# The gated recurrence of block two takes decay and value from the layer-norm rows by a combined matrix, instead of from the projected input

## The chip, the cores and the metric

One core of a Trainium2 chip runs the whole program. The metric is device microseconds of one launch. Three runs of the kernel before took 937.53, 940.71 and 940.95 us; the median is 940.71 us.

## What is computed

Two pre-norm decoder blocks on x (16 sequences x 128 tokens x 128 features), each with a recurrence, a cross-attention and a feed-forward part. The change sits in the recurrence of block two and borrows time in the feed-forward part of block one (eight experts and a shared one). Cut to what matters, the recurrence is:

```python
def _L1_attn_ref(x, omega, Win, Wl, bl, Wv, bv, Wout):      # x is the layer norm of the residual
    xz = jnp.einsum('btd,ed->bte', x, Win)
    xi, z = jnp.split(xz, 2, axis=-1)                       # 256 features each
    log_lam = -C * softplus(omega) * sigmoid(jnp.einsum('bti,ji->btj', xi, Wl) + bl)
    lam = jnp.exp(log_lam)
    v = jnp.einsum('bti,ji->btj', xi, Wv) + bv
    h0 = xi[:, 0]
    def step(h_prev, inp):
        x_t, v_t, lam_t = inp
        vh = jnp.sum(v_t * h_prev, axis=-1, keepdims=True)
        vv = jnp.sum(v_t * v_t, axis=-1, keepdims=True)
        Qh = h_prev - 2.0 * v_t * (vh / vv)
        h = lam_t * Qh + (1.0 - lam_t) * x_t
        return (h, h)
    ...
    return jnp.einsum('bti,di->btd', silu(z) * h, Wout)
```

## The kernel before, in words

Everything lies in SBUF with features on the 128 partitions. The 2048 token rows form four groups g of 512. The five engines each run one hand-written order of instructions and meet by counting semaphores.

**Rounded products.** Where single precision is wanted at the fast rate, a matrix is kept in two parts of type fp32r, an upper part (a rounded copy) and a lower part (the rest). A product is then three fast ones (PARTS: upper x upper, upper x lower, lower x upper) accumulated in PSUM. `up` (L1751) does this with the parts of the layer-norm rows in `xhl` and of the weights in `whl`. Plain fp32 products of 128x512 show as two records each.

**The expert loop of block one** (TensorE, ScalarE and VectorE each loop over i = 0 to 35: nine feed-forward networks times four groups). A step is four times `up` (12 fast products), Silu on ScalarE (`silu_up`, L821), the gate product on VectorE (`hidden`, L1300), upper and lower part of the hidden rows (`hidden_upper` L828, `hidden_lower` L1308), and the down product of the step before (`down_T`, L1925, 6 fast products; L1744 in steps 4 to 7 and 32 to 35). VectorE also adds the weighted outputs (L1317, L1322). TensorE waits in step i for the Silu and gate product of step i - 1, bank by bank. PSUM banks 0 to 5 are used; 6 and 7 serve the router and the last transposes.

**The stage before the recurrence** (this is what the change reorders). The last layer norm of the block runs group by group: `normalize(3, g)` (L664) on ScalarE and L1056 on VectorE, `transpose_xn(3, g)` on TensorE into bank g, `copy_xnT(3, g)` (L673, upper part) on ScalarE and `ln_lower` (L1064, lower part) on VectorE. Then:

- `xz(g)`: 12 fast products into banks 4 to 7, one bank per 128 features (the first half is xi, the second z). `xz_copy(g)` (L860) on ScalarE copies each to SBUF.
- `lam_or_v` (L1999): from xi in SBUF, full fp32, two products of contraction 128 for each 128 output features; v goes to banks 0 and 1, lambda to 2 and 0. It waits for the first two `xz_copy` of its group.
- ScalarE: v with its bias (L875), its square (L880), tanh (L883) and exp (L887) for lambda. Tanh is in the table that Silu left; exp isn't, so a table load stands before the first exp.
- `v_dot_v(g)` (L2011) sums the squares into bank 3; VectorE takes the reciprocal (L1415); `spread_reciprocal(g)` (L2017) brings it to all partitions, again in bank 3.
- VectorE, for each group: nb = (lambda - 1) * xi (L1418), w = -2 v / vv (L1421), w * lambda (L1424), then `chain_products(g)` (L1378 to L1385): products of lambda, v and w over the positions 1 to 3 of chunks of four tokens. For g = 1 it writes into R[2], which lies on rows of `xhl`, and so waits until all 16 products of xz are done.
- GpSimd, for each group: local sums gl, their products with v (L552 to L566). For g = 1 it waits for all 16 `xz_copy`.
- `chunk_dots(g)` (L2035, L2039): sums of the chain products over features into banks 4 to 7 (0 to 3 for g = 3). The first waits for all 16 `xz_copy`. ScalarE copies a part (`e_copy`, L868); VectorE's `solve(g)` (L1401 to L1409) follows, one group behind its chain products.

TensorE's order today is xz(0), then for g = 0 to 3: v and lambda of g, v_dot_v(g), spread_reciprocal(g); behind g = 0 come xz(1) and xz(2), behind g = 1 xz(3) and the dots of group 0, and so on. The recurrence itself (32 chunks, L1470 to L1486 with L2078) follows.

## Time and profile before

| | |
|---|---|
| median of three runs | 940.71 us (937.53 to 940.95) |
| the profiled execution, its span | 947.1 us, 6.4 us above that median; the page gives nothing around the span |
| busy, of the span | TensorE 812.7 us (86%), weight loads 583.1 (62%), VectorE 768.9 (81%), ScalarE 524.0 (55%), GpSimd 492.0 (52%) |
| expert loop of block one | about 300 to 466 us |
| stage before the recurrence | 471.7 us to about 556 us |
| recurrence of block two | about 556 to 626 us |
| costliest group | L1751, 576 fast products, 145.3 us busy |
| L1308, lower part of the hidden rows | 56 instructions, 806 ns mean |

How to read it: a share of busy time is an average over stages with different limits, so the chain that ended last (which piece of work released the next) is read together with the timelines of the engines in the two stretches. TensorE's records overlap, so the time from one start to the next says more than the length of one. The granted clock is a share of TensorE's full speed.

### The profile page before, as it was taken

How to read it: one execution, taken by the hardware profiler on the slowest of the kernel's cores; microseconds unless marked ns; L12 is line 12 of the kernel's file. 1: busy time of each engine (PE TensorE's matmuls, PEld its weight loads, DVE VectorE, ACT ScalarE, POOL GpSimd, SP SyncE). 2: the span in 40 equal slices, each digit the busy share in tenths (PEclk: the TensorE clock that was granted, in tenths of full speed). 3: DMA queues.
4: the chain of work that ended last, by engine and by line, in shares of the span. 5: the costliest groups of instructions: out<-in, count | busy, mean ns of one | idle time of the engine just before them, and what ended most of it. 6: DMA issues, size and time to landing. Idle time of an engine off the chain costs nothing.

```text
span 947.1 us, 14667 instructions
## 1 busy us (share of the span) xinstructions
PE 812.7 (86%) x5061; PEld 583.1 (62%) x5061; DVE 768.9 (81%) x1419; ACT 524.0 (55%) x960; POOL 492.0 (52%) x490
## 2 busy tenths in 40 slices
PE   7958777777798999999999867799999899899891
PEld 6433232322266888887866555577766678789781
DVE  5588999999987489999848988886799978857663
ACT  5966666666637635554364232226565684078771
POOL 6358999999962021222248833456344310077773
PEclk9968999999998899999999999999799999999996
DMA  7000000000000031323000000000000031096554
GB/s 205 1 0 1 0 1 1 0 1 0 0 1 1 12 114 62 106 79 106 0 2 1 1 0 1 1 1 1 1 2 25 24 89 47 14 163 173 152 128 158
DMA packets 36739, 39.67 MB, mean 42 GB/s; under 512 B 5131, under 2 KB 28697, under 8 KB 35898
## 3 DMA queue, kind: packets, MB, share of 16 engines
q1 hardware_dynamic: 34170, 33.62, 11.8%
q0 software_dynamic: 2496, 5.12, 3.3%
q8 instruction: 40, 0.66, 0.3%
q14 instruction: 33, 0.27, 0.1%
HBM read 30.86 MB, written 7.86 MB: 41 GB/s over the span
## 4 chain that ended last, share of the span: by engine, by line
PE 39%; DVE 19%; ACT 5%; issue 5%; POOL 4%; DMA 3%; POOLq 0%; ACTq 0%; SPq 0%; DVEq 0%
PE ps L1751 10%; PE ps L1925 3%; PE ps L1744 3%; PE ps L2132 2%; DMA G<-xn_rows,token 2%; PE ps L1999 2%; PE ps L2267 2%; POOL y_rows L640 2%; DVE small L1520 2%; PE ps L2122 1%; PE ps L2276 1%; PE ps L2078 1%; DVE R L1481 1%; PE ps L1799 1%; DVE G L1523 1%
## 5 line engine op out<-in xcount | busy, mean ns | idle before, releaser
L1751 PE MATMUL ps<-xhl,whl 128*128 128x512 f32 x576 | 145.3, 402 | 5.3 <-ACT G L701 2.6
L1751 PEld LDWEIGHTS ps<-xhl,whl 128*128 128x128 f32 x576 | 109.0, 193 | 30.1 <-issue 5.7
L476 POOL TENSOR_TENSOR R<-G,R 128x1024 f32<-128x1024 f32 x43 | 100.8, 2360 | 28.9 <-ACT R L707 22.5
L1189 DVE TENSOR_TENSOR_SCAN R<-ps,R 128x1024 f32<-128x1024 f32 x43 | 97.5, 2278 | 5.5 <-POOL R L485 5.5
L749 ACT ACTIVATE ps<-G,negAb,negA 128x508 f32<-128x508 f32 x128 | 95.0, 779 | 2.6 <-DVE R L1189 2.6
L1778 PE MATMUL ps<-bc,sel 96*128 96x512 bf16 x128 | 47.1, 396 | 51.5 <-ACT LN L714 22.1
L1799 PE MATMUL ps<-R,ident 128*128 128x512 f32 x172 | 83.1, 605 | 0.0
L1778 PEld LDWEIGHTS ps<-bc,sel 96*128 96x128 bf16 x128 | 12.5, 99 | 104.7 <-ACT LN L714 35.8
L707 ACT COPY R<-ps 128x512 f32<-128x512 f32 x64 | 37.5, 585 | 71.1 <-PE ps L1778 71.1
L821 ACT ACTIVATE G<-ps 128x512 f32<-128x512 f32 x72 | 42.8, 599 | 56.7 <-PE ps L1751 56.6
L440 POOL TENSOR_TENSOR rstd<-small,mhalf 128x4 f32<-128x4 f32 x24 | 25.7, 1069 | 86.4 <-DVE small L1050 86.4
L635 POOL DMA_INDIRECT G<-xn_rows,token x39 | 39.4, 1010 | 58.9 <-DVE per_tile L1683 45.4
L1300 DVE TENSOR_TENSOR G<-G,ps 128x512 f32<-128x512 f32 x72 | 48.6, 681 | 17.1 <-ACT G L821 16.2
L445 POOL CAST whl<-ew 128x512 fp32r<-128x512 f32 x9 | 5.8, 646 | 106.5 <-DMA ew<-in_w_dram 106.4
L965 ACT COPY G<-ps 120x512 f32<-120x512 f32 x64 | 34.9, 589 | 42.0 <-PE ps L2132 42.0
L1693 DVE TENSOR_TENSOR G<-ps,biasT 128x512 f32<-128x512 f32 x39 | 26.9, 690 | 34.8 <-PE ps L2267 34.7
L1799 PEld LDWEIGHTS ps<-R,ident 128*128 128x128 f32 x172 | 32.5, 194 | 29.1 <-issue 24.0
L1189 DVE TENSOR_TENSOR_SCAN LN<-ps,LN 128x1024 f32<-128x1024 f32 x21 | 47.9, 2280 | 2.7 <-POOL LN L485 2.1
L476 POOL TENSOR_TENSOR LN<-G,R 128x1024 f32<-128x1024 f32 x21 | 49.8, 2373 | 0.1
L1729 PE MATMUL ps<-ident 128*128 128x128 f32 x326 | 42.8, 291 | 5.8 <-DVE G L1407 3.3
L1308 DVE TENSOR_TENSOR hl<-G,hl 128x512 fp32r<-128x512 f32 x56 | 44.6, 806 | 1.9
L1729 PEld LDWEIGHTS ps<-ident 128*128 128x128 f32 x326 | 40.9, 206 | 7.2 <-DVE G L1407 3.9
(376 smaller groups left out, 2162.8 us busy)
## 6 DMA issues: line engine op xcount, KB each, us to landing
R<-in_exp_wi_dram SPq DMA_DIRECT2D x39, 256.0 KB, 3.5
G<-cw_by_expert SPq DMA_DIRECT2D x6, 1024.0 KB, 4.6
ew<-in_w_dram SPq DMA_DIRECT2D x24, 128.0 KB, 2.2
y_rows<-zeros SPq DMA_DIRECT2D x1, 2048.0 KB, 9.3
xn_rows<-LN SPq DMA_DIRECT2D x8, 256.0 KB
G<-in_exp_wo_dram SPq DMA_DIRECT2D x8, 256.0 KB, 4.7
G<-y_rows SPq DMA_DIRECT2D x4, 512.0 KB, 5.5
X<-in_x_dram SPq DMA_DIRECT2D x4, 256.0 KB, 4.6
```

Of the source, the lines that this page charges most:

```text
L476: gp.tensor_tensor(halves(dBu[i % 3]), duT[:, :, gcols(i // NS)], Bsb[:, i % 4:i % 4 + 1, :].broadcast_to([P, HI, GT]), ALU.mult).then_inc ...
L635: gp.indirect_dma_start(x_at(i), None, xn_dram[:, :], bass.IndirectOffsetOnAxis(ap=token[:, i:i + 1], axis=0))\
L707: sc.copy(Bsb[:, i % 4, :], bank(4)[:, 0, :]).then_inc(S["b_copied"], 1)
L749: sc.activation(bank(2 * j + m)[:, 0, :].rearrange("p (b t) -> p b t", b=GB)[:, :, 1:T], dT[:, m, gcols(g)].rearrange("p (b t) -> p b t", ...
L821: sc.activation(sh[:, i % 2, m * GT:(m + 1) * GT], bank(m)[:, 0, :], ACT.Silu).then_inc(S["silu0"], 1)
L1189: v.tensor_tensor_scan(hst[i % 3], bank(2 * j, 2).rearrange("p h n -> p (h n)"), dBu[i % 3], 0.0, ALU.mult, ALU.add).then_inc(S["scanned"], 1)
L1300: v.tensor_tensor(hidr[:, i % 2, m * GT:(m + 1) * GT], sh[:, i % 2, m * GT:(m + 1) * GT], bank(2 + m)[:, 0, :], ALU.mult).then_inc(S["hid0 ...
L1308: v.tensor_tensor(hl[:, i % 2, 1, m * GT:(m + 1) * GT], hidr[:, i % 2, m * GT:(m + 1) * GT], hl[:, i % 2, 0, m * GT:(m + 1) * GT].bitcast( ...
L1729: mm(bank(o)[:, 0, 0:P], ident[:], ident[:], start=True, stop=True)
L1751: ins = mm(mix(out) if n == N_WIN1 else out, whl[:, wslot(n), i, m * P:(m + 1) * P], rhs, start=k == 0, stop=k == 2)
L1778: mm(bank(bank_i)[:, 0, :], sel[:, r, :], bc3[:, gcols(g)], start=True, stop=True).then_inc(S[s], 1)
L1799: ins = mm(bank(6 + m)[:, 0, :], ident[:], hC[i % 3][:, m * GT:(m + 1) * GT], start=False, stop=i % NS == NS - 1, skip_group_check=True)
```

## The change

- Before the loop's end, a combined matrix is made: the first half of the input projection (Win's xi rows) is transposed on TensorE at step 11 into bank 7, ScalarE copies it (step 12), TensorE multiplies it with Wv and Wl at step 13 in full fp32 (four products of 128x256) into bank 6, ScalarE writes the upper part (step 14) and VectorE the lower (step 15). The result `lvhl` (128 x 2 parts x 512) takes the place of weights of block one that are no longer needed.
- v and lambda are three fast products of `lvhl` with `xhl` for each 128 features, and no longer wait for xz or its copies; they wait for the group's layer-norm parts and their banks.
- The order of TensorE and ScalarE in the stage is new. VectorE's nb now waits for the group's xi copies. The table with exp and tanh is loaded ahead of the last normalizations.

```diff
...
 DRIVE = 4
 NDRIVE = NC // DRIVE
 FIRST_ROUND = (10, 18, 26)
+LV_AT = 11
 POOL_HC = (1, 4, 7, 10, 13)
 EB = 4
 NT = 2 * N // P + E - 1
...
         nones, nselu = diagD[:, 0, :], diagD[:, 1, :]
         rvv = sb("rvv", [P, NG, C4])
 
+        with nc.sbuf_tensor("lvhl", [P, 2, 2 * DI], F32R) as lvhl:
+            pass
+
         w = {}
         for name, shape in (
             ("W_in", [P, 4, P]), ("W_delta", [P, HI, DI]), ("b_delta", [P, HI]), ("W_BC", [P, HI, 2 * NS]),
...
         wo_now = R[:, 3, :, :].rearrange("p s (w n) -> p (s w) n", w=2)
 
 
+        Win1T = LN[:, 1, 0:HI * P].rearrange("p (k n) -> p k n", k=HI)
+
         S = {}
         for name in (
             "x_in0", "x_in1", "x_in2", "x_in3", "w_win", "w_mamba", "w_ctx", "w_lru", "w_att", "w_gate", "w_e0a", "w_e0b",
...
 
         FIRST = {}
         for name, shared, count in (
+            ("wt1_mm", "cwt_mm", 1), ("wt1_ev", "rt_exp", 1), ("lv_mm", "rt_mm", 1), ("lv_hi", "rt_cw", 1), ("lv_lo", "rt_sub", 1),
             ("bc_up", "w_upper", 1), ("bc_rem", "diag_ready", HI), ("sp_log", "omega_sp", 1),
             ("t_mm", "l_mm", HI * NG), ("cnt_mm", "vt_mm", NG), ("lst_mm", "vv_mm", NG), ("bt_mm", "dots_mm", 2 * NG), ("wo_cp", "z_silu", 2 * HI), ("ebo_mm", "hk_mm", NG),
             ("xt_ev", "l_ev", HI * NG), ("bt_ev", "lam_done", HI * NG), ("ebo_ev", "v2_ev", HI * NG),
...
                 if i == 2 * NG - 1:
                     act.wait_ge(S["cwt_mm"], 1)
                     sc.copy(cw_rows, bank(6)[:, 0, 0:T]).then_inc(S["cw_rows"], 1)
+                if i == LV_AT + 1:
+                    wait(act, "wt1_mm", 1)
+                    sc.copy(Win1T, bank(7)[:, 0, 0:HI * P].rearrange("p (k n) -> p k n", k=HI)).then_inc(S["wt1_ev"], 1)
+                if i == LV_AT + 3:
+                    wait(act, "lv_mm", 1)
+                    sc.copy(lvhl[:, 0], bank(6)[:, 0, :]).then_inc(S["lv_hi"], 1)
                 if i == 3:
                     act.wait_ge(S["rt_sub"], 1)
                     sc.activation(router[:, 1, :, :], router[:, 0, :, :], ACT.Exp).then_inc(S["rt_exp"], 1)
 
+            sc.preload_act_table_set("exp_and_others")
             for g in range(NG):
                 normalize(3, g)
                 if g == NG - 2:
...
                 act.wait_ge(S["dots_mm"], 2 * g + 2)
                 sc.copy(row(cp, g)[:, 1:C4], e_psum(g).rearrange("p (i k) -> p i k", k=KG)).then_inc(S["e_ev"], 1)
 
-            xz_copy(0)
             copy_xnT(3, NG - 1)
-            for g in range(NG):
+
+            def v_copy(g):
                 for m in range(HI):
                     act.wait_ge(S["v2_mm"], HI * g + m + 1)
                     sc.activation(row(vv[:, m], g), mix(bank(m)[:, 0, :]), ACT.Identity, bias=w["bv"][:, m:m + 1])\
                         .then_inc(S["v2_ev"], 1)
+
+            def v_square(g):
                 act.wait_ge(S["v2_ev"], HI * (g + 1))
                 if g >= 2:
                     act.wait_ge(S["vt_mm"], g - 1)
                 sc.activation(sq[:, g % 2], pos(vv, g), ACT.Square).then_inc(S["sq_done"], 1)
+
+            def decays(g):
                 for m in range(HI):
                     act.wait_ge(S["l_mm"], HI * g + m + 1)
                     sc.activation(row(lam[:, m], g), mix(bank(2 - 2 * m)[:, 0, :]), ACT.Tanh, bias=coef[:, 0, m:m + 1], scale=0.5)\
...
                     act.wait_ge(S["l_ev"], HI * g + m + 1)
                     sc.activation(row(lam[:, m], g), row(lam[:, m], g), ACT.Exp, bias=coef[:, 2, m:m + 1], scale=coef[:, 2, m:m + 1])\
                         .then_inc(S["lam_done"], 1)
-                if g == 0:
-                    xz_copy(1)
-                    xz_copy(2)
-                if g == 1:
-                    xz_copy(3)
-                if g >= 1:
-                    carry_last(g - 1)
-                    e_copy(g - 1)
+
+            for g in range(NG):
+                v_copy(g)
+                if g < NG - 1:
+                    v_square(g)
+                decays(g)
+                xz_copy(g)
+            carry_last(0)
+            e_copy(0)
+            v_square(NG - 1)
+            for g in range(1, NG - 1):
+                carry_last(g)
+                e_copy(g)
             carry_last(NG - 1)
             e_copy(NG - 1)
             for m in range(HI):
...
                 elif i == NG + 1:
                     compare(probs, range(E // 2, E))
                     step(v.tensor_reduce(router[:, 2], pair[:, 0], AX.X, ALU.add))
+                if i == LV_AT + 4:
+                    wait(dve, "lv_hi", 1)
+                    v.tensor_tensor(lvhl[:, 1], bank(6)[:, 0, :], lvhl[:, 0].bitcast(F32), ALU.subtract).then_inc(S["lv_lo"], 1)
                 if 0 <= i - E * NG + 1 < NG:
                     add_YT(i - E * NG + 1)
                 if i > E * NG:
...
                 v.reciprocal(rvv[:, g, :], bank(3)[:, 0, 0:C4 * VW:VW]).then_inc(S["rvv_done"], 1)
                 dve.wait_ge(S["lam_done"], HI * (g + 1))
                 step(v.memset(lam_g[:, :, 0, 0:GB], 0.0))
+                dve.wait_ge(S["xz_ev"], 4 * g + HI)
                 v.scalar_tensor_tensor(pos(nb, g), lam_g, 1.0, pos(xi, g), ALU.subtract, ALU.mult).then_inc(S["nb_done"], 1)
                 dve.wait_ge(S["nb_done"], g + 1)
                 dve.wait_ge(S["vv_mm"], g + 1)
...
                 if i == 2 * NG - 1:
                     pe.wait_ge(S["rt_cw"], 1)
                     nc.tensor.transpose(bank(6)[:, 0, 0:T], router[:, 5].rearrange("p b e -> p (b e)"), ident[:]).then_inc(S["cwt_mm"], 1)
+                if i == LV_AT:
+                    pe.wait_ge(S["w_lru"], 16 * 6)
+                    for k in range(HI):
+                        ins = nc.tensor.transpose(bank(7)[:, 0, k * P:(k + 1) * P], w["Win1"][:, k, :], ident[:])
+                    ins.then_inc(S["wt1_mm"], 1)
+                if i == LV_AT + 2:
+                    wait(pe, "wt1_ev", 1)
+                    for j, name in enumerate(("Wv", "Wl")):
+                        for k in range(HI):
+                            ins = mm(bank(6)[:, 0, j * DI:(j + 1) * DI], Win1T[:, k, :], w[name][:, k, :], start=k == 0, stop=k == HI - 1)
+                    ins.then_inc(S["lv_mm"], 1)
                 if i - 1 in by_feature:
                     down_T(i - 1)
                 elif i >= 1:
...
             pe.wait_ge(S["w_split"], N_WIN1 + 1)
 
             def xz(g):
-                pe.wait_ge(S["ln_lo"], 2 * NG + g + 1)
-                if g == 0:
-                    pe.wait_ge(S["res0"], (E + 1) * NG)
                 for m in range(4):
                     if g:
                         pe.wait_ge(S["xz_ev"], 4 * g - 3 + m)
                     up(bank(4 + m)[:, 0, :], N_WIN1, m, g).then_inc(S["xz_mm"], 1)
 
-            def lam_or_v(g, wt, banks, done, freed):
+            def lam_or_v(g, first, banks, done, freed):
 
                 for m in range(HI):
                     if freed[m][1] > 0:
                         pe.wait_ge(S[freed[m][0]], freed[m][1])
-                    for k in range(HI):
-                        ins = mm(mix(bank(banks[m])[:, 0, :]), wt[:, k, m * P:(m + 1) * P], row(xi[:, k], g),
-                                 start=k == 0, stop=k == HI - 1)
+                    elif banks[m]:
+                        pe.wait_ge(S["ln_lo"], 2 * NG + banks[m] + 1)
+                    cols = slice((first + m) * P, (first + m + 1) * P)
+                    for k, (i, j) in enumerate(PARTS):
+                        ins = mm(mix(bank(banks[m])[:, 0, :]), lvhl[:, i, cols], row(xhl[:, j], g), start=k == 0, stop=k == 2)
                     ins.then_inc(S[done], 1)
+
+            def lam_and_v(g):
+                pe.wait_ge(S["ln_lo"], 2 * NG + g + 1)
+                lam_or_v(g, 0, (0, 1), "v2_mm", (("l_ev", HI * g), ("v2_ev", HI * g)))
+                lam_or_v(g, HI, (2, 0), "l_mm", (("l_ev", HI * g - 1), ("v2_ev", HI * g + 1)))
 
             def v_dot_v(g):
                 pe.wait_ge(S["sq_done"], g + 1)
...
                     ins = mm(e_psum(g), ones[:], ep[g % 2][:, k], start=k == 0, stop=k == HI - 1)
                 ins.then_inc(S["dots_mm"], 1)
 
+            wait(pe, "lv_lo", 1)
+            pe.wait_ge(S["res0"], (E + 1) * NG)
+            transpose_xn(3, NG - 1)
+            lam_and_v(0)
             xz(0)
-            transpose_xn(3, NG - 1)
-            for g in range(NG):
-                pe.wait_ge(S["xz_ev"], 4 * g + HI)
-                if g == 0:
-                    pe.wait_ge(S["ln_lo"], 2 * NG + 3)
-                lam_or_v(g, w["Wv"], (0, 1), "v2_mm", (("l_ev", HI * g), ("v2_ev", HI * g)))
-                lam_or_v(g, w["Wl"], (2, 0), "l_mm", (("l_ev", HI * g - 1), ("v2_ev", HI * g + 1)))
+            v_dot_v(0)
+            spread_reciprocal(0)
+            lam_and_v(1)
+            xz(1)
+            v_dot_v(1)
+            lam_and_v(2)
+            xz(2)
+            lam_and_v(3)
+            xz(3)
+            spread_reciprocal(1)
+            chunk_dots(0)
+            for g in range(2, NG):
                 v_dot_v(g)
                 spread_reciprocal(g)
-                if g == 0:
-                    xz(1)
-                    xz(2)
-                if g == 1:
-                    xz(3)
-                if g:
-                    chunk_dots(g - 1)
+                chunk_dots(g - 1)
             chunk_dots(NG - 1)
 
             def s_known(c):
```

## Rows read from the trace of the kernel before

**Rows 1.** The chain that ended last, pieces in order: start us, us, what
```profile
413.88 2.72 PE ps L1751 x12
416.60 1.36 PE ps L1925 x6
...
471.72 3.01 PE ps L1751 x12
...
475.17 6.87 PE ps L1999 x16
482.04 1.75 PE ps L2011 x16
...
484.04 1.16 PE ps L2017 x8
485.20 5.46 PE ps L1751 x24
...
504.13 2.87 PE ps L2035 x12
```

**Rows 2.** Busy time by stretch, core 0: us, each engine's busy us, granted clock, DMA
```profile
376.00:399.00 23.00, 23.00 (x104) 19.02 (x103) 22.45 (x35) 13.39 (x24) 3.84 (x4) 1.00 0.21 67
534.00:535.00 1.00, 1.00 (x8) 1.00 (x9) 1.00 (x1) 0.00 (x0) 0.00 (x0) 0.70 0.00 0
535.00:536.00 1.00, 1.00 (x4) 0.70 (x4) 0.55 (x2) 0.00 (x0) 0.73 (x1) 0.50 0.00 0
538.00:540.00 2.00, 2.00 (x11) 1.59 (x10) 1.97 (x2) 0.00 (x0) 1.90 (x2) 1.00 0.00 0
```

**Rows 3.** Timeline of VectorE: start us, us, line, operation, [idle before, releaser]
```profile
385.23 2.59 DVE L1308 TENSOR_TENSOR hl<-G,hl 128x512 fp32r<-128x512 f32 x2
...
485.76 1.23 DVE L1418 SCALAR_TENSOR_TENSOR G<-G 128x1024 f32<-128x1024 f32 x1
...
499.29 0.18 DVE L1415 RECIPROCAL rvv<-ps 128x4 f32<-128x4 f32 x1 [2.69 <-PE ps L2011]
...
501.27 1.22 DVE L1421 SCALAR_TENSOR_TENSOR G<-G,ps 128x1024 f32<-128x1024 f32 x1
...
503.86 0.96 DVE L1378 TENSOR_TENSOR R<-G 128x768 f32<-128x768 f32 x1
...
516.92 0.18 DVE L1415 RECIPROCAL rvv<-ps 128x4 f32<-128x4 f32 x1 [1.26 <-PE ps L2011]
...
518.71 1.22 DVE L1421 SCALAR_TENSOR_TENSOR G<-G,ps 128x1024 f32<-128x1024 f32 x1
...
521.47 1.36 DVE L1378 TENSOR_TENSOR ew<-G 128x768 f32<-128x768 f32 x1
...
535.51 1.22 DVE L1421 SCALAR_TENSOR_TENSOR G<-G,ps 128x1024 f32<-128x1024 f32 x1 [0.45 <-PE ps L2017]
```

**Rows 4.** Timeline of ScalarE in the second block
```profile
461.34 0.87 ACT L664 ACTIVATE LN<-X,stats,rstd 128x128 f32<-128x128 f32 x2
...
467.91 1.05 ACT L673 CAST xhl<-ps 128x512 fp32r<-128x512 f32 x2
...
472.75 2.60 ACT L860 COPY G<-ps 128x512 f32<-128x512 f32 x4 [1.52 <-PE ps L1751]
...
482.78 1.28 ACT L887 ACT_TABLE_LOAD   x1
...
512.48 1.06 ACT L880 ACTIVATE LN<-G 128x1024 f32<-128x1024 f32 x1
...
515.19 0.69 ACT L883 ACTIVATE G<-ps,coef 128x512 f32<-128x512 f32 x1 [1.03 <-PE ps L1999]
515.78 1.50 ACT L887 ACTIVATE G<-G,coef 128x512 f32<-128x512 f32 x2
```

**Rows 5.** Timeline of TensorE in the second block
```profile
465.01 0.82 PE L1737 MATMUL ps<-ident,LN 128*128 128x128 f32 x6
...
533.83 1.57 PE L2017 MATMUL ps<-ident,rvv 128*128 128x128 f32 x8 [3.02 <-DVE rvv L1415]
```

## The prediction, made before the changed kernel was run

> **What bounds the kernel now.** I read the chain that ended last first, then the busy time by stretch, then the timelines of TensorE, ScalarE, VectorE and GpSimd between 456 and 556 us. Two places matter, because the change adds work in one and reorders the other.
>
> The first is the expert loop of block one (steps i = 0 to 35). From i = 9 on, the chain is TensorE alone: 12 products of L1751 in 2.72 us, then 6 of L1925 in 1.36 us, so a step every 4.08 us [rows 1]. TensorE is busy 23.00 of 23.00 us there, VectorE 22.45, ScalarE 13.39 [rows 2]. Work put on TensorE here moves the end by its own length.
>
> The second is the stage before the recurrence of block two, from 471.72 [rows 1] to about 556 us. For each of four groups TensorE makes xz (12 rounded products, 2.73 us, half of the 5.46 us for two groups), then v and lambda (L1999, 16 records, 6.87 us), the sums of squares (L2011, 1.75 us) and the spread reciprocal (L2017, 1.16 us) [rows 1]. Until 515 us the chain lies almost wholly on TensorE, after that on VectorE. Once fed, VectorE stops only briefly: 1.26 us before the reciprocal of group 2 and 0.45 us before w of group 3 [rows 3].
>
> **The change, part by part.**
>
> (a) Expert loop, TensorE. Four transposes took 0.44 us (475.17 less 471.72 + 3.01 [rows 1]), so the two at i = 11 cost 0.22. At i = 13, four full-precision products 128 columns by 256 are 8 records. A 512-column record of L1999 takes 6.87/16 = 0.43 us, so a 256-column one takes 0.215 us, and eight take 1.72 us [rows 1]. Sum 1.94 us, all on the path. Bounds: 0 if TensorE had slack (the stretch shows none), 2.6 if the switches between forms cost 0.1 us each. I take 1.95.
>
> (b) Expert loop, other engines. ScalarE gets two copies of about 0.6 us; it is idle 9.6 us in 23 [rows 2], and the copies stand behind its last work of a step, so nothing. VectorE gets one subtraction of about 0.7 us. It is nearly full [rows 2], but when GpSimd stretched two of its ops to 2.59 us [rows 3], 1 us over their mean on the page, TensorE kept its step; and TensorE has just stood 1.94 us longer, which VectorE gains as slack. I take 0; if that cover were gone, 0.7.
>
> (c) The table load. Today it stands between tanh and exp of group 0, 1.28 us [rows 4]. It moves ahead of the first normalization, which starts at 461.34 us and takes 0.87 [rows 4]. That one then ends near 463.6 instead of 462.2 us; its transposes start at 465.01 us behind other products [rows 5]. Cost 0.
>
> (d) The order of the stage. v and lambda become 3 rounded products for each 128 rows, as in xz: 2.73 us a group in place of 6.87, so 4 x 4.14 = 16.6 us leave TensorE. Were TensorE the only limit, that would be the gain. It isn't: three waits stand in the new code. The spread reciprocal of group 1 is issued after xz of group 3. VectorE's chain products of group 1 wait for all 16 xz products, since they write where the rows xhl lie. The first dots wait for all 16 copies of xz, since they use the same banks. So I lay out the new times on the old clock.
>
> TensorE is free at 471.4. Transposes of group 3 take 0.44 us, so lambda and v of group 0 run 471.85 to 474.6, xz to 477.35, squares and the wait for VectorE's reciprocal take 2.0 us (482.04 to 484.04), the spread 1.16 [rows 1]: 480.5. The first v of group 1 is in ScalarE's hands at 481.3.
>
> ScalarE then sets the pace. One group is two v activations (0.6 and 0.7, as tanh), the square (1.06), two tanh (0.69, but 0.59 from one start to the next, 515.19 to 515.78), two exp (1.50) [rows 4], and four copies of xz. The four took 2.60 us where TensorE delivered one each 0.68 us; two copies that lay ready took 1.05 us together, so four ready ones take 2.1 [rows 4]. A group is 7.0 us (7.5 with the slow copies). Two groups on from 481.3, with a small wait on TensorE at group 2: 495.65. Its first v activation of group 3 ends at 496.3 and frees bank 0; then TensorE makes the last lambda product (0.68), xz of group 3 (2.73, ends 499.75) and the spread (1.16). VectorE can start w of group 1 at **501.0**. It starts at 501.27 today [rows 3]. With 7.5 us a group it would be 502.0.
>
> So VectorE, which begins group 0 near 479.6 instead of 485.76 (it needs the reciprocal at 479.4 and xi), has finished that group at 490.4 and nb of group 1 at 492, and stands idle for 9 us. The 16.6 us saved on TensorE are mostly a wait.
>
> From w of group 1 on VectorE is again the bound. Today 501.27 to 515.66 us (516.92 less its wait of 1.26), 14.4 us [rows 3]. Its ops that ran while GpSimd was idle will now run beside it, for GpSimd starts group 1 once all xz copies are out, as the first dots do: near 502 us, and not at 504.1 [rows 1]. The first chain product took 0.96 us there against 1.36 us beside GpSimd in group 2 [rows 3], and the product before it can lose some 0.3 (estimate from that pair). So 14.4 + 0.7 = 15.1, and group 2's reciprocal comes at 516.1 against 516.92.  Now something new is late: TensorE has had nothing since about 508 us, 8 us of idleness.
>
> (e) The clock. Today group 3's spread follows 3.02 us of idleness and takes 1.57 us for 1.16 [rows 5]; the granted clock is 0.70 in its last part, then 0.50 [rows 2]: the 1.2 GHz level. VectorE waits 0.45 us for that spread [rows 3]. In the new order group 2's spread comes after 8 us of idleness. At full clock w of group 2 starts near 517.4, with a spread twice as slow (2.3 us) at 518.6; today 518.71 [rows 3]. Group 3 can lose another 0.5 us in the same way. The whole stage changes by -1.3 to +1.0 us; I take **-0.4**, between the two, as only the last part of today's spread ran slow. The Trainium skill (TensorE: Matmul & The Clock Gate, Part 1) has the engine at 1.2 GHz by default and released by activity; by it both spreads run at half clock from the start, and the stage comes out at +0.5. Trace and page differ on the first part of that spread only.
>
> The dots of groups 1 to 3 (2.87 us for 12 records [rows 1], about 4 for all 16) run beside VectorE's chain products and have some 4 us of room before its solve, so they cost nothing unless the clock stays low. The recurrence behind the stage is untouched: TensorE is warmed for it by the same products.
>
> Sum: +1.95 - 0.4 = **+1.6 us** on this execution, whose span of 947.1 us lies 6.4 us above the median of the three runs (940.71); nothing beside the span is shown for it, so I carry the difference over: 942.3.
>
> **Rivals.**
>
> R1, VectorE stays fed. If, against my reading, VectorE could run group 1 straight behind group 0, the stage would end earlier by its 6.15 us head start and by its later stalls (2.69 + 1.26 + 0.45 = 4.4 [rows 3]): -10.6 + 1.95 = -8.6, 932.1. For it: that is what shorter products would do, and v and lambda stand on today's chain with 6.87 us a group. Against it: both waits of (d) are in the code, and even a stage bound by TensorE alone (eight times 2.73, two rounds of squares, one spread, the transposes) ends xz of group 3 at 498.4, so w of group 1 not before 499.6. Chance 0.09.
>
> R2, slower: the low clock lasts. It decides if TensorE stays at 1.2 GHz through the dots of groups 1 and 2 and not for about 3 us as today. Then dots take 8 us instead of 4 and use up their room. Two spreads cost 1.2 us more each, two dots up to 0.5 each, and VectorE's subtraction of (b) 0.7, against 1.0 us saved ahead of them: 1.95 + 2.4 + 1.0 + 0.7 - 1.0 = +5, 945.8. For it: TensorE's busy share falls from near full to half in the stage. Against it: from 538 us on the clock is back at 1.00 today [rows 2]. Chance 0.12.
>
> R3, the added products are hidden, or take no time, in the expert loop: -0.4, 940.3. Against it, a chain that is all TensorE. Chance 0.07.
>
> Forecast as above: 0.72.
>
> **How the numbers follow.** About 0.5% (4.7 us) is what a measurement of this kernel can tell from no change. My own case spans -1.3 + 1.9 = +0.6 to 1.0 + 2.7 = +3.7 us; a start of w 1 us later takes it to +4.7, and the runs before lie 3.4 us apart, so its upper end is 945.5. The 8 in 10 range reaches down through R3 to 938.8 and up to 946.0, into R2. Faster: R1, 0.09. Slower: R2, 0.12. Within: 0.79.
>
> **What would show it.** In the profile after: 8 records of about 0.215 us between two steps of the loop, and the loop 1.95 us longer (wrong if the steps absorb them); no table load between tanh and exp; VectorE's first op of group 0 some 6 us earlier on the stage's clock, and a gap of 8 to 10 us ahead of w of group 1, released by the spread reciprocal; the first dots within 2 us of today's place; granted clock 0.5 somewhere in the spreads of groups 2 and 3. The prediction is wrong if that gap is under 4 us, or if ScalarE isn't dense from 481 to 499 us.

## The result, and the profile after

The changed kernel took 947.24 us (median of four executions, 946.35 to 948.34), the kernel before 939.38 us beside it (937.53 to 940.95). The ratio is 1.0085, with an interval of 1.0064 to 1.0105: 7.9 us slower. I had forecast 942.3 us, and a range that ends at 946.0. The profiled execution has a span of 944.9 us (946.65 us with what lies around it), shorter than the 947.1 us of the trace I had read of the kernel before. That is the first thing to explain, and it is taken up behind the table below.

What I had laid out by hand is in the trace nearly as written. First the added work in the expert loop, in the timeline of TensorE (start us, us, line, operation):

```profile
351.98 2.89 PE L1778 MATMUL ps<-xhl,whl 128*128 128x512 f32 x12
354.70 0.38 PE L1992 MATMUL ps<-ident,w_Win 128*128 128x128 f32 x2
354.84 1.64 PE L1952 MATMUL ps<-hl,w2hl 128*128 128x512 f32 x6
...
363.12 1.02 PE L1998 MATMUL ps<-w_Wv,LN 128*128 128x256 f32 x4
363.98 1.03 PE L1998 MATMUL ps<-w_Wl,LN 128*128 128x256 f32 x4
364.66 1.74 PE L1952 MATMUL ps<-hl,w2hl 128*128 128x512 f32 x6
```

The first set of four records takes 0.86 us from its start to the start of the next (363.12 to 363.98). A record is 0.215 us, as worked out, and TensorE never stops around them.

Then the stage, as TensorE saw it (the same view, 468 to 533 us):

```profile
468.88 0.63 PE L1764 MATMUL ps<-ident,LN 128*128 128x128 f32 x4
469.26 3.02 PE L2037 MATMUL ps<-xhl,lvhl 128*128 128x512 f32 x12
472.13 2.89 PE L1778 MATMUL ps<-xhl,whl 128*128 128x512 f32 x12
...
490.92 2.26 PE L2037 MATMUL ps<-xhl,lvhl 128*128 128x512 f32 x9
493.87 0.96 PE L2037 MATMUL ps<-xhl,lvhl 128*128 128x512 f32 x3 [0.69 <-ACT G L889]
494.67 2.89 PE L1778 MATMUL ps<-xhl,whl 128*128 128x512 f32 x12
497.39 1.05 PE L2059 MATMUL ps<-ident,rvv 128*128 128x128 f32 x8
498.94 2.87 PE L2077 MATMUL ps<-ew,ones 128*128 128x384 f32 x12 [0.50 <-ACT G L874]
...
513.62 2.07 PE L2059 MATMUL ps<-ident,rvv 128*128 128x128 f32 x8 [8.78 <-DVE rvv L1441]
...
530.79 2.08 PE L2059 MATMUL ps<-ident,rvv 128*128 128x128 f32 x8 [8.15 <-DVE rvv L1441]
```

v and lambda of a group now take 2.87 us from start to start, for 6.87 before [rows 1]. The last lambda product waits for ScalarE, as reckoned. And TensorE stands idle for 8.78 and 8.15 us ahead of the last two spread reciprocals, which take 2.07 and 2.08 us; in the kernel before the last one took 1.57 [rows 5]. VectorE (its timeline, same columns) shows what that does:

```profile
477.03 1.23 DVE L1445 SCALAR_TENSOR_TENSOR G<-G 128x1024 f32<-128x1024 f32 x1
...
498.55 1.22 DVE L1448 SCALAR_TENSOR_TENSOR G<-G,ps 128x1024 f32<-128x1024 f32 x1 [8.97 <-PE ps L2059]
...
501.34 1.30 DVE L1404 TENSOR_TENSOR R<-G 128x768 f32<-128x768 f32 x1
...
513.39 0.17 DVE L1441 RECIPROCAL rvv<-ps 128x4 f32<-128x4 f32 x1
...
515.80 1.22 DVE L1448 SCALAR_TENSOR_TENSOR G<-G,ps 128x1024 f32<-128x1024 f32 x1 [0.95 <-PE ps L2059]
```

It waits 8.97 us in front of w of group 1; I had said 9. From the transposes of group 3 to that w are 29.7 us; I had said 501.0 less 471.4 = 29.6. The granted clock is still 1.00 when TensorE falls idle, goes to 0.50 within each idle stretch and stays there through the spread:

```profile
503.00:508.00 5.00, 1.83 (x17) 1.69 (x15) 4.86 (x6) 1.73 (x3) 4.69 (x6) 1.00 0.00 0
508.00:518.00 10.00, 4.38 (x12) 3.22 (x13) 8.76 (x16) 0.00 (x0) 8.24 (x12) 0.50 0.00 1
518.00:525.00 7.00, 4.64 (x29) 3.82 (x27) 6.83 (x7) 0.78 (x2) 6.76 (x7) 0.98 0.00 0
525.00:535.00 10.00, 4.21 (x12) 3.22 (x13) 8.76 (x16) 0.00 (x0) 6.88 (x10) 0.50 0.00 0
```

(Busy time by stretch of the changed kernel, columns as in rows 2.) So nothing in the stage accounts for 7.9 us. Cut into parts, by the starts of the same products in each trace, the two executions compare so:

| trace | expert loop, from the down product of step 8 to the last one | from there to the last layer norm's transposes | stage, to the first recurrence product | recurrence | attention heads of block two, first to last score product |
|---|---|---|---|---|---|
| before, the trace read for the prediction | 95.30 | 18.56 | 91.70 | 62.47 | 106.49 |
| changed | 97.16 | 18.81 | 91.78 | 62.46 | 106.45 |

The change costs 1.86 + 0.25 + 0.08 = 2.2 us. In these two traces the heads are alike. What I did not know is that 106.5 us is not what they take at their best. The trace of before already showed the clock low in them (busy time by stretch, columns as in rows 2; its first score product starts at 653.50 us):

```profile
653.50:660.50 7.00, 5.01 (x43) 3.71 (x42) 6.82 (x9) 3.46 (x5) 7.00 (x11) 1.00 0.00 1
660.50:667.50 7.00, 6.91 (x53) 4.70 (x54) 6.35 (x6) 3.57 (x6) 2.33 (x6) 0.51 0.01 2
667.50:674.50 7.00, 7.00 (x56) 5.19 (x55) 2.17 (x4) 2.66 (x4) 2.56 (x6) 0.51 0.00 0
```

Why is the changed execution the shorter one all the same? Its down product of step 8 starts at 346.54 us, that of before at 351.15, and up to there the two kernels do the same. From the down product of step 1 to that of step 8 the changed kernel's trace takes 39.30 us and that of before 42.49. In the latter the clock was at 0.50 from 316 to 322 us. The router's products and the down product behind them show it, in TensorE's timeline of before:

```profile
312.86 4.01 PE L1914 MATMUL ps<-w_router,LN 128*128 128x8 f32 x32
316.73 2.91 PE L1925 MATMUL ps<-hl,w2hl 128*128 128x512 f32 x6
```

and in that of the changed kernel:

```profile
311.45 3.63 PE L1941 MATMUL ps<-w_router,LN 128*128 128x8 f32 x32
314.94 1.63 PE L1952 MATMUL ps<-hl,w2hl 128*128 128x512 f32 x6
```

In the 20 traces of this case this piece has one of three lengths, whatever the kernel: 39.3 to 39.4 us in seven, 40.9 to 41.0 in six, 42.5 to 42.6 in seven. So executions of one program reach the later stages up to 3.2 us apart by this alone.

In four of the five later sets of runs the routed experts at the end, in which TensorE waits for token rows brought by DMA (8.1 us in all in h2's trace), took 118 to 130 us from their first product on TensorE to their last, instead of 95 to 97, and scattered, so the times there are near 967 us and are only compared with the kernel before beside them.

### The profile page after: what moved, and what is told of

Read it like the earlier page. It is cut to its first block, busy times and chain, and to the rows that moved or that the text cites. A ratio compares the mean times of both kernels' runs of the same rounds, so it can differ in the third digit from the quotient of the medians.

```text
span 944.9 us, 14658 instructions
## 1 busy us (share of the span) xinstructions
PE 792.9 (84%) x5055; PEld 577.0 (61%) x5055; DVE 771.4 (82%) x1420; ACT 521.3 (55%) x962; POOL 493.4 (52%) x490
## 4 chain that ended last, share of the span: by engine, by line
PE 32%; DVE 24%; issue 6%; ACT 5%; POOL 5%; DMA 2%; POOLq 0%; DVEq 0%; ACTq 0%
PE ps L1778 7%; PE ps L1771 3%; POOL y_rows L647 2%; PE ps L2177 2%; DVE G L1323 2%; PE ps L2167 2%; DVE small L1547 2%; POOL G L642 2%; PE ps L1952 2%; PE ps L2312 2%; DVE G L1550 1%; PE ps L2123 1%; DVE R L1508 1%; DMA G<-xn_rows,token 1%; PE ps L1826 1%
## 5 line engine op out<-in xcount | busy, mean ns | idle before, releaser
L1778 PE MATMUL ps<-xhl,whl 128*128 128x512 f32 x576 | 143.0, 397 | 6.0 <-ACT G L708 2.6
L483 POOL TENSOR_TENSOR R<-G,R 128x1024 f32<-128x1024 f32 x43 | 100.8, 2359 | 26.7 <-ACT R L714 20.4
```

Source lines behind the costliest of these rows:

```text
L483: gp.tensor_tensor(halves(dBu[i % 3]), duT[:, :, gcols(i // NS)], Bsb[:, i % 4:i % 4 + 1, :].broadcast_to([P, HI, GT]), ALU.mult).then_inc ...
L1778: ins = mm(mix(out) if n == N_WIN1 else out, whl[:, wslot(n), i, m * P:(m + 1) * P], rhs, start=k == 0, stop=k == 2)
```

## The experiments

### First set: before again, the matrix alone, the spread earlier, the load where it was

**b1**, the kernel before, unchanged. 

> The kernel before, unchanged, profiled again. Theory S (the stage and the expert loop behave as the trace of before showed, but that one execution was itself slow somewhere outside them): the span comes out near 938 us, the stage from the last transposes to the first recurrence chunk takes the same 85 us as in the first trace of before, and the 8 to 10 us between the traces lie elsewhere. Rival T (the first trace was typical in its shape, and before's other executions are shorter in the stage): the stage itself is several us shorter than 85 us here.

Measured 967.37 us against 966.91 (1.0013, 0.998 to 1.0045). In its trace the loop takes 95.28 us, the stage 91.73, the heads 106.51. Theory S holds for the stage, and rival T falls (with before's order the stage takes 91.5 to 92.3 us in all five traces). But the heads are long again, so this trace doesn't yet show where before's usual executions are shorter.

**e1**, the kernel before with the combined matrix made and not used. Cut to the two places on TensorE:

```diff
+                if i == LV_AT:
+                    ...
+                if i == LV_AT + 2:
+                    ...
```

> The combined matrix is made in the expert loop as in the changed kernel, but not used; the stage is that of before. Theory A (TensorE is the chain in the loop, the work is on it): 1.95 us over before, within 1.5 to 2.7. Rival L (the added work sets TensorE's clock or the engines' phase off and costs several times its length somewhere later): 5 us or more over before, with a lower mean clock.

Measured 1.0027 (0.9991 to 1.0064), or 2.6 us with 3.5 either way. The trace is sharper: the loop takes 97.14 us, 1.86 more than b1. The stage takes 92.31 us, 0.6 more than in b1, though its code is that of before. And the heads take 98.41 us, 8.1 less, in code that nothing touched.

**e2**, the changed kernel with one line moved.

```diff
             xz(2)
+            spread_reciprocal(1)
             lam_and_v(3)
             xz(3)
-            spread_reciprocal(1)
```

> The changed kernel, with the spread reciprocal of group 1 issued ahead of lambda and v of group 3 and not behind xz of group 3. By the trace of the changed kernel VectorE waits about 8 us for it, and its chain products of group 1 wait for xz of group 3 alone. Theory A: w of group 1 and its product with lambda leave the path, the stage ends 3 to 4 us sooner than in the changed kernel: about 943.5 us. Rival: another wait (dots or solve of group 0) takes its place, and the gain is under 1 us.

Measured 0.9944 (0.991 to 0.9978) of before. The stage is 87.60 us, 4.2 under the changed kernel. VectorE's timeline (same columns):

```profile
492.30 1.22 DVE L1448 SCALAR_TENSOR_TENSOR G<-G,ps 128x1024 f32<-128x1024 f32 x1 [2.48 <-PE ps L2059]
...
497.81 0.96 DVE L1404 TENSOR_TENSOR R<-G 128x768 f32<-128x768 f32 x1 [2.59 <-PE ps L1778]
```

The wait of 8.97 us became two, of 2.48 us for the spread and of 2.59 us for xz of group 3. This was theory A.

**e3**, the changed kernel without the early table load.

```diff
-            sc.preload_act_table_set("exp_and_others")
```

> The changed kernel without the early load of the exp and tanh table, so that the load stands again between tanh and exp of group 0. Theory A: ScalarE is dense to xz of group 3, so the stage grows by at most 1.3 us over the changed kernel, unless its first wait of 0.7 us for group 1 absorbs part: 947.5 to 948.5 us. Rival L (what is lost lies in the loop's end, where the early load delays the layer norm): no change or a gain against the changed kernel.

The stage stays at 91.78 us. ScalarE waits 0.27 us for the first v of group 1 and not 1.70 us: that wait had room for the load, so the early load gains nothing and costs nothing. Yet the kernel measured 1.0073 of before (1.0033 to 1.0112), and eight of its ten executions had a mean granted clock of 0.940 to 0.945 (seven of these took 970 to 979 us), the other two 0.950 and 0.952 at 967 and 965 us. Its trace is one of the latter, with heads of 98.41 us. Executions like the seven are called the long kind below. That their heads took 106.5 us is a guess for all that have no trace.

### Second set: are the heads the place?

TensorE has two gaps at the start of the heads, while VectorE and ScalarE work on the first scores. The edit fills them; `unread(bank, n)` issues n full fp32 products of 128 x 128, whose results nobody reads:

```diff
             head_scores(0, 1)
+            unread(4, 3)
             pe.wait_ge(S["hq_lo"], NG)
-            unread(7, 8)
+            unread(7, 13)
```

**f1**, the changed kernel again. 

> The changed kernel, unchanged, against before on one chip, with a second profile. Theory C (the change itself costs about 0.9 us of schedule, and the rest of the 7.9 us was the attention heads of block two starting at the 1.2 GHz level, 106.5 against 98.4 us, which this kernel's executions meet more often than those of before): the ratio lies between 1.001 and 1.009, and its runs split by mean clock, about 0.01 apart. Rival R (the 7.9 us are in the change's own stage and the traces hide it): the ratio is 1.0085 again and the runs do not split.

1.0058 of before (1.0027 to 1.0089), median 972.0 us. The traced execution took 964.58 us with heads of 98.43 us at a mean clock of 0.950; the other eleven took 970 to 978 us, at clocks of 0.934 to 0.947.

**f2**, the changed kernel with the fill. 

> The changed kernel with eight more unread products on TensorE in the two gaps at the start of the attention heads (3 before the wait for the last query part, 13 in place of 8 behind it). Theory C: the heads take 98.4 to 99 us in the profile and the median falls by up to 8 us against the changed kernel. Rival: the clock falls all the same and the heads take 106 us or more.

0.9993 (0.9959 to 1.0028): 4.2 us under f1. In the trace the clock holds at the start of the heads and is at 0.50 later, from 725 to 730 us; they take 101.1 us.

**f3**, the kernel before with the fill. 

> The kernel before with the same eight more products. Theory C: its heads take 98.4 to 99 us; it gains at most as much as before's executions met the low clock there, and stands 0.9 us under the changed kernel with the same products (a ratio of the two of 1.001). Rival R: the changed kernel stays 5 us or more behind it.

0.9969 (0.9939 to 0.9999), heads 100.8 us. The two filled kernels stand 2.6 us apart, close to the 2.2 us of schedule, where the unfilled ones stood 5.7 apart. Rival R falls, and the stage of 91.8 us in every trace of the changed kernel says the same. The heads did not come down to the forecast 99 us in either: by the times the fill helps the changed kernel (f2 against f1), and it doesn't cure.

**f4**, fill and early spread. 

> Both: the early spread reciprocal of group 1 and the eight more products. Theory A with C: the stage 4.1 us shorter than in the changed kernel and the heads at 98.4 to 99 us; the fastest of all, 3 us or more under before with the same products.

0.9941 (0.991 to 0.9973), stage 87.62 us, heads 99.7 us. It is the fastest of the set, 2.5 us under f3, where 3 or more had been expected.

### Third set: is it the moment at which the heads come?

The edit is idle products on TensorE at step 15 of the expert loop, in front of everything in question: `unread(7, 4)`, `(7, 5)`, `(7, 9)`.

**g1**, the kernel before with 0.9 us more. 

> The kernel before with four unread products (8 records, 0.9 us) more on TensorE at step 15 of the expert loop: as much longer, up to the heads, as the changed kernel's trace is. Theory P (whether the attention heads start at the 1.2 GHz level hangs on the moment at which they come, and the change moved them by about 0.9 us): it is slow like the changed kernel, 4 us or more over before, with a mean clock about 0.005 lower. Rival Q (the slow heads come from what the changed order does in its stage, its idle TensorE and its low clock there): 0.9 us over before and no more.

0.9992 (0.9964 to 1.002): theory P missed, and so did the 0.9 us, which the scatter on this chip hides (the loop is 0.92 us longer in the trace, the heads 101.1 us).

**g2**, the changed kernel with 1.1 us more. 

> The changed kernel with five unread products (1.1 us) more at step 15. Theory P: most of its executions get past the low clock in the heads, so it is 3 to 7 us faster than the changed kernel beside it although it does 1.1 us more work. Rival Q: 1.1 us slower than the changed kernel.

0.9999 (0.9972 to 1.0025), 967.75 us, and no execution at a clock under 0.948. The changed kernel beside it (g4) stood at 975.7 us. With more work it was 8 us faster by the median (5.5 by the mean), and its trace has heads of 98.39 us; rival Q says slower by 1.1.

**g3**, with 2.05 us more. 

> The changed kernel with nine unread products (2.05 us) more at step 15. Theory P: as the one with five, or between it and the changed kernel. Rival Q: 2 us slower than the changed kernel.

1.0035 (1.0011 to 1.0059), clocks from 0.943 to 0.955: between g2 and g4. Its traced execution took 974.01 us at a clock of 0.943, which looks like the long kind, and yet its heads took 98.41 us. Its down product of step 8 started at 351.80 us, 3.3 us behind that of g2's trace. So in these scattered sets neither the time nor the mean clock of an execution tells what its heads did.

**g4**, the changed kernel. 

> The changed kernel unchanged, as the reference on this chip. Theories P and Q alike: 4 to 8 us over before; the loop's 97.1 us and the stage's 91.8 us in the profile as in the two traces before, and heads of either 98.4 or 106.5 us.

1.0054 (1.0014 to 1.0095). Five of eight executions took 975 to 979 us at clocks of 0.938 to 0.942, the other three 963 to 969 us at 0.950 to 0.953. The traced one is of these, with heads of 98.41 us.

### Fourth set: TensorE kept busy in the stage

**h1** and **h2**, two more traces of the changed kernel, in a set as quiet as the first measurement. 

> A further profile of the changed kernel. If it falls among the slow executions (mean clock about 0.942), theory C expects the loss in the attention heads (106.5 for 98.4 us) with loop 97.1 and stage 91.8 us as before; rival Q expects the stage or the recurrence to be longer than 91.8 and 62.5 us.

> As the one before it: theory C, any loss against 98.4 us is in the heads; rival Q, in the stage or the recurrence.

h1 took 942.72 us with heads of 100.94 us and a mean clock of 0.952; h2 took 940.77 us with 98.41 us and 0.961. Loop and stage are alike in both (97.1 and 91.8 us). The kernel before had 939.94 us beside them (17 executions, 937.65 to 941.20, clocks 0.962 to 0.967).

**h3**, the changed kernel with its two idle stretches filled.

```diff
             for g in range(2, NG):
                 v_dot_v(g)
+                unread(0, 34)
                 spread_reciprocal(g)
```

> The changed kernel with 34 unread products on TensorE in each of its two idle stretches of 8 us ahead of the spread reciprocals of groups 2 and 3. In the profile both spreads run at full clock and VectorE's waits of 0.95 us for them go: the stage is 1 to 2 us shorter (theories P and Q alike). Theory Q (idleness and low clock of the stage bring the slow executions on): the slow group vanishes, 5 us or more under the changed kernel, at or under before. Theory P (it is the moment at which the heads come that decides): the median moves by the 1 to 2 us and by whatever the shift does, in either direction.

939.10 us, 0.9993 of before (0.9983 to 1.0002), twelve executions between 937.75 and 940.92 us, clocks 0.962 to 0.969. TensorE's timeline:

```profile
509.24 7.81 PE L1756 MATMUL ps<-ident 128*128 128x128 f32 x68
518.21 1.16 PE L2059 MATMUL ps<-ident,rvv 128*128 128x128 f32 x8 [1.16 <-DVE rvv L1441]
...
534.60 1.16 PE L2059 MATMUL ps<-ident,rvv 128*128 128x128 f32 x8 [1.97 <-DVE rvv L1441]
```

Both spreads are back at 1.16 us, the stage is 90.25 us, 1.5 less, and no execution is of the long kind; its trace has heads of 98.41 us. But neither h1 nor h2, all there is of the changed kernel beside it, was of that kind. So the set shows the 1.5 us of the stage, and that before's time is reached; that h3 took the long kind away follows only against the first measurement.

**h4**, early spread, filled stage (19 products ahead of group 2's spread, 34 ahead of group 3's) and filled heads. 

> Early spread reciprocal of group 1, TensorE kept busy in the stage, and the eight more products at the heads. Theory A with C: stage 86 to 87 us, heads 98.4 to 100 us, no slow group, and 0.6 to 0.9% faster than before.

935.68 us, 0.9961 of before (0.9948 to 0.9974): 4.3 us under the kernel before, stage 86.84 us, heads 98.40 us. The forecast of 0.6 to 0.9% was too high.

### Last set: busy TensorE, same moment

**i1**, h3 with seven products (1.6 us) at step 15, so that the heads come when they do in the changed kernel. 

> The changed kernel with TensorE kept busy in the stage (34 unread products twice) and seven unread products (1.6 us) more at step 15 of the expert loop, so that the heads come at the moment at which they come in the changed kernel. Theory Q (idleness and low clock of the stage bring the slow heads on): still no slow group, 1.6 us over the version without the seven products. Theory P (the moment decides): the slow group is back, and the median is within 2 us of the changed kernel.

**i2**, the changed kernel beside it. 

> The changed kernel beside it. Both theories: 4 to 8 us over before, executions in two groups by clock.

i1 measured 965.76 us, 1.0035 of before (1.0004 to 1.0066), i2 970.27 us (1.0056, 1.0027 to 1.0085). i1 scatters again: six executions of 961 to 965 us, six of 966 to 972, with no gap between them; its trace has a stage of 90.23 us and heads of 100.90. That is not the even kernel that theory Q expects, and its median is 4.5 us under i2's, not within the 2 us of theory P. With ranges of 10.6 and 12.0 us in twelve executions each, this set does not decide between them.

i2's trace caught an execution with long heads in the changed kernel, beside one with short heads (h2). Its execution took 973.35 us at a mean clock of 0.940, one of the long kind, and its loop, stage and recurrence are 97.11, 91.79 and 62.46 us, as in all the others. The heads take 106.51 us. Busy time from their first product on, i2:

```profile
652.30:659.30 7.00, 5.00 (x43) 3.70 (x42) 6.82 (x9) 3.47 (x5) 7.00 (x11) 1.00 0.00 1
659.30:666.30 7.00, 6.91 (x53) 4.68 (x54) 6.35 (x6) 3.56 (x6) 2.33 (x6) 0.51 0.01 2
666.30:673.30 7.00, 7.00 (x56) 5.18 (x55) 2.18 (x4) 2.66 (x4) 2.54 (x6) 0.51 0.00 0
673.30:680.30 7.00, 7.00 (x108) 5.20 (x112) 5.47 (x8) 4.83 (x8) 2.59 (x6) 1.00 0.01 2
```

and the same 28 us of h2, the same program:

```profile
653.30:660.30 7.00, 5.03 (x43) 3.71 (x42) 6.82 (x9) 3.43 (x4) 7.00 (x11) 1.00 0.00 1
660.30:667.30 7.00, 6.33 (x90) 4.63 (x94) 6.69 (x7) 5.35 (x9) 3.49 (x10) 1.00 0.01 2
667.30:674.30 7.00, 7.00 (x116) 5.38 (x109) 5.86 (x7) 4.08 (x7) 3.59 (x8) 1.00 0.01 2
674.30:681.30 7.00, 6.90 (x102) 5.20 (x102) 6.88 (x9) 4.71 (x8) 3.00 (x7) 1.00 0.00 0
```

After the same seven microseconds with TensorE 5.0 us busy, one execution goes on at 1.00 and the other at 0.51, nearly all of it at the 1.2 GHz level, for the next 14 us. There TensorE is full and issues about half as many records, and VectorE, nearly full in h2, is left waiting: 2.2 us busy in the third stretch instead of 5.9. Single groups of products show it too. These are two lines of TensorE's timeline in the changed kernel's first trace; just before, the same kinds of products, as many of them, took 0.92 and 1.09 us:

```profile
658.11 1.54 PE L2167 MATMUL ps<-kz,qhl 32*128 32x480 f32 x6
659.61 1.96 PE L2177 MATMUL ps<-ident,G 128*120 128x128 f32 x8
```

## Why the prediction was wrong

**(a), the added products: right.** 1.86 us for 1.95, and no switch between forms cost anything that shows. **(b)**, the copies and the subtraction at nothing: right, the loop grew by TensorE's part alone. **(c)**, the table load: right that it costs nothing where it went, and it saved nothing where it left (e3), because ScalarE had a wait of 1.70 us to hide it in. The 0.25 us between loop and transposes come with the matrix (18.81 us in e1 too, 18.57 in b1); their cause was not looked for.

**(d), the order: right.** The start of w, the 8.97 us of idleness and ScalarE's pace were in the trace to 0.1 us, and e2 showed what the wait for the spread had cost: moved forward by one line it gave 4.2 of the 16.6 us by which TensorE's products had become shorter. (By the lengths as the prediction lists them, ScalarE's group adds up to 7.2 us and not 7.0; from start to start it took 7.1 on average.) R1 fell, as its waits are real: even in e2 VectorE waits 2.59 us for xz of group 3.

**(e), the clock in the stage: right in kind, a little small.** The spreads took 2.07 and 2.08 us, and VectorE waited 0.95 us for each (h3 brought both back to 1.16 us and took 1.5 us off the stage). The stage came out at +0.1 us, for my -0.4: w of group 2 came 0.4 us earlier than before, as seen from the start of the stage, and the longer wait for group 3's spread, 0.95 for 0.45 us, took that back. The upper bound of +1.0 us does not follow from its own terms, which give +0.4. The Trainium skill's rule (TensorE: Matmul & The Clock Gate, Part 1) was the better guide here: by it both spreads run at half clock from the start, and they did.

The sum of these is +2.2 us, for my +1.6. An execution of the changed kernel whose heads were not slowed took 940.77 us, and before took 939.94 us beside it.

**The step that failed is that all behind the stage was put at nothing, with "The recurrence behind the stage is untouched" as its only reason.** The recurrence is (62.46 for 62.47 us), but I ended the search there. The heads, 97 us behind the stage, took 98.4 us at their best and 106.5 us when the clock fell to its lower level at their start. In the two quiet sets (the first measurement and the fourth set) the times say that this is common in the changed kernel and rare in the one before: the former took 946.35 us or more in four of six executions, the latter 941.20 us or less in all 21, and only the execution traced for the prediction was longer. The traces by themselves don't: with the kernels unchanged, the heads were long in both traces of before and in two of six of the changed kernel (98.4 us in three, 100.9 in one). The rival R2 named the right cause, a low clock that lasts, at the wrong place: it priced it in the stage.

**A second step was weak: how the execution stands to the median.** I noted that the profiled span lay 6.4 us above the median of the runs, and wrote "I carry the difference over" without asking where it was. It was in the heads. That trace had 106.49 us in a kernel whose usual time has room for 98.4 only. Had I looked at the clock of the stretches behind the stage, the lower level at the start of the heads would have stood out, and its price could have been estimated. As it was, 942.3 us came near to the executions whose heads were not slowed so (940.77 and 942.72 us), which is what it had been worked out for.

Do the other executions of the first measurement fit? They have no traces. Their mean clocks, 0.951, 0.950 and 0.953, are like that of the trace with long heads (0.953), but h1 has 0.952 with heads of 100.94 us, so the clock doesn't decide it. Their times do better: 946.4 to 948.3 us, beside 946.65 for the trace, and 3.6 to 5.6 us above h1. With h2's 940.8 us and heads longer by 8.1 one gets 948.9 us, from which the pieces ahead of step 8 can take some 2 us, as in the trace. So all four probably had the loss; this is argued and not shown.

**What stays open** is why the change would make this fall of the clock common. Two things seem to move it. With 1.1 us more work ahead of the heads no execution had a clock under 0.948 (g2, against five of eight under 0.943 in g4). With TensorE kept busy in the stage none was long (h3, against the first measurement), but they scattered when the time was given back (i1). 0.9 us more in the kernel before did not bring the long kind (g1), and that kernel meets long heads at times by itself (b1 and the first trace). It may be a matter of when the heads come, of what TensorE did before, or of both; 18 runs did not settle it. A shift by a fixed amount is also a blunt test, as executions of one program differ by up to 3.2 us ahead of step 8 by themselves. The changed kernel had long heads with 39.3 and 39.4 us there (its first trace, i2), and short ones with 39.3 us too (g4). A test of many executions of one kernel with traces of each was not made.

## What to carry to other kernels

Before adding a change to a profile, ask where the profiled execution differs from the median; a stage that can run at either clock level can be worth more than the edit (here 8.1 us, against 4.2 for the best of the moves), and in a trace the level stands beside each stretch. Shorter products gained nothing here while a wait in the program order stood behind them: move the small instruction that others wait for ahead of the long ones. Where TensorE is left waiting for several microseconds in front of a product on the path, products that nobody reads are cheap, but look at the stages behind too, since g2 suggests that a shift of 1 us can change the clock they get.

## What was not expected of the hardware

The same 7 us of work in the heads, ahead of the same products, were followed by the full clock in one execution and by the lower one in another (i2 and h2), and the lower one lasted 14 us although TensorE was full all along. Elsewhere (today's spread of group 3 [rows 2]) it came back within about 3 us. And with more work ahead, 1.1 us of it, the kernel was 8 us faster by the median (967.75 against 975.69 us on one chip).
